# Self and cross attention of a layer as one pipeline of 32 groups, with the query parts on the GpSimd queue

## The reference

```
h  = ln(x) * (1 + scale) + shift            # self attention
q, k, v = split(h @ W_qkv + b)
x += gate * (softmax(q k^T * D**-0.5) v @ W_proj + b)
q  = ln(x) @ W_q + b                        # cross attention, keys and values from the context
k, v = split(context @ W_kv + b)            # layer 1 normalises the context first
x += softmax(q k^T * D**-0.5) v @ W_cproj + b
x += gate_m * mlp(ln(x) * (1 + scale_m) + shift_m)
```

## Time and profile before

| what | value |
|---|---|
| median of 3 runs | 3974.96 us (3955.16 to 3978.48) |
| the profiled execution | 3992.97 us, span 3991.2 us |
| mean granted clock of TensorE | 0.885 of full speed |
| busy: PE, PEld, DVE, ACT, POOL | 83%, 52%, 70%, 54%, 28% |
| DMA, HBM over the span | 164.42 MB moved, HBM 5 GB/s |
| packed attention of layer 1 (self, cross) | 1526 to 1934 us, 1934 to 2338 us |
| packed attention of layer 2 (self, cross) | 2491 to 2899 us, 2900 to 3317 us |

### The profile page before, as it was taken

One profiled execution on the slowest core, in us unless ns is written; L12 is line 12 of the kernel. 1 busy time (PEld: TensorE's weight loads), 2 busy tenths in 40 slices (PEclk: granted clock), 3 DMA queues, 4 the chain that ended last, 5 costly groups with the idle time before them and its releaser, 6 DMA issues. The chain is left out here.

```text
span 3991.2 us, 100093 instructions
## 1 busy us (share of the span) xinstructions
PE 3311.6 (83%) x31675; PEld 2059.8 (52%) x31675; DVE 2802.8 (70%) x12631; ACT 2146.6 (54%) x5112; POOL 1120.2 (28%) x1448
## 2 busy tenths in 40 slices
PE   3999867777777796898699977798879997788998
PEld 2454434444444474555466655465546665545555
DVE  5677689999999784887367568588646757764333
ACT  1566545555555573666256555376625655533443
POOL 2000056666666562111111135111011214410000
PEclk9999978988888796999599879699858978898999
DMA  4000000000000002343134300343223420000000
GB/s 119 13 11 11 11 8 8 8 7 7 8 7 6 1 0 52 98 104 89 45 95 97 83 4 0 81 104 100 59 68 86 100 66 1 22 18 10 14 13 13
DMA packets 138546, 164.42 MB, mean 41 GB/s; under 512 B 40982, under 2 KB 87574, under 8 KB 137750
## 3 DMA queue, kind: packets, MB, share of 16 engines
q1 hardware_dynamic: 119286, 128.40, 12.7%
q0 software_dynamic: 10240, 21.84, 2.4%
q10 hardware_dynamic: 8608, 9.18, 0.9%
HBM read 13.87 MB, written 4.19 MB: 5 GB/s over the span
## 5 line engine op out<-in xcount | busy, mean ns | idle before, releaser
L635 ACT ACTIVATE topk_prob<-topk_s,topk_nmx 128x77 f32<-128x77 f32 x1024 | 248.2, 326 | 320.5 <-POOL topk_nmx L531 213.7
L1224 ACT ACTIVATE cross_pT<-cross_t 77x512 f32<-77x512 f32 x512 | 275.7, 589 | 201.3 <-PE cross_t L1469 201.0
L1333 DVE TENSOR_REDUCE self_mx<-self_s 128x4 f32<-128x512 f32 x512 | 328.8, 684 | 67.5 <-PE self_s L1454 65.1
L1224 ACT ACTIVATE self_pT<-self_t 128x512 f32<-128x512 f32 x512 | 279.0, 600 | 138.9 <-PE self_t L1469 138.9
L1333 DVE TENSOR_REDUCE cross_mx<-cross_s 128x4 f32<-128x308 f32 x512 | 220.3, 472 | 141.2 <-PE cross_s L1454 140.4
L537 POOL TENSOR_SCALAR topk_mask<-topk_work 128x308 f32<-128x308 f32 x256 | 251.5, 983 | 228.1 <-DVE topk_work L778 227.8
L926 PE MATMUL topk_t<-ident,topk_prob 128*77 128x128 f32 x1024 | 189.5, 316 | 147.2 <-POOL topk_prob L541 146.8
L926 PEld LDWEIGHTS topk_t<-ident,topk_prob 128*77 128x77 f32 x1024 | 136.4, 170 | 264.0 <-ACT topk_pT L621 122.2
L916 PE MATMUL topk_s<-kbd,topk_qT 128*128 128x308 f32 x512 | 218.0, 511 | 51.1 <-ACT topk_prob L635 47.4
L1686 POOL TENSOR_TENSOR mlp_hid<-mlp_hid 128x512 fp32r<-128x512 f32 x160 | 210.4, 1315 | 156.1 <-DVE mlp_hid L1759 108.0
L1454 PEld LDWEIGHTS cross_s<-packed_keys,packed_queries 32*128 32x128 f32 x2048 | 159.7, 217 | 133.9 <-issue 80.2
(11 more groups left out here) (333 smaller groups left out, 8710.5 us busy)
## 6 DMA issues: line engine op xcount, KB each, us to landing
packed_keys<-self_kT SPq DMA_DIRECT2D x384, 64.0 KB, 2.1
packed_queries<-self_qT SPq DMA_DIRECT2D x384, 64.0 KB, 2.1
packed_queries<-cross_qT SPq DMA_DIRECT2D x384, 64.0 KB, 2.2
packed_queries<-zero_rows SPq DMA_DIRECT2D x128, 128.0 KB, 2.7
packed_keys<-cross_kT SPq DMA_DIRECT2D x384, 39.0 KB, 1.9
kbd<-window_kT SPq DMA_DIRECT2D x512, 8.0 KB
kbd<-topk_kT SPq DMA_DIRECT2D x512, 4.8 KB
packed_queries<-self_om POOLq DMA_DIRECT2D x128, 64.0 KB, 2.2
```

What stands on the lines that cost most here:

```text
L635: last = nc.scalar.activation(prob[:, u % 4, h * keys:(h + 1) * keys], s_ps[:, u % 2, h * keys:(h + 1) * keys], ACT.Exp, scale=SCALE, bias ...
L1224: nc.scalar.activation(pT[0:keys, c % 2, h, :], t_ps[0:keys, h, :], ACT.Exp, scale=SCALE).then_inc(s_exp, 1)
L1333: nc.vector.tensor_reduce(mx[:, (c // 2) % 2, 2 * k + h, :], sc, AX.X, ALU.max).then_inc(s_max, 1)
```

## The change

`packed_attention_phase(nc, r, layer, kind)` becomes `packed_attention_layer(nc, r, layer)`. One block holds both attentions: there are NT = 32 groups, of which 0 to 15 are the self attention and 16 to 31 the cross attention of the same sequences. `at(n)` gives for a group which attention it is and its number within it. The number of iterations is 32 + 3 where it was 16 + 3 twice.

The query parts move from the SP queue to the GpSimd queue. They are issued in slot 7 of iteration i for group i + 2, behind `stage_context`, and therefore ahead of the `send_maximum` of slot 0 of the next iteration. SP keeps the keys.

On PE, `outputs_to_rows` and `values_times_probs` of the even slots move from right behind the scores to the end of the slot, behind the projections and the unread matmuls. The odd slots keep their order. In the prologue the layer norm of groups 1 and 2 starts before the low parts and the values of the group before it are done. The layer norm statistics of a cross group wait for the addition of the self attention of the same group. The tile of the low and high keys always has the width of the self attention.

```diff
-def packed_attention_phase(nc, r, layer, kind):
+def packed_attention_layer(nc, r, layer):
...
+    NT = 2 * NG
+    def at(n):
+        return (cross_a if n >= NG else self_a), n % NG
...
-            for i in range(NG + 3):
-                body(i, i % 3, i, NG - i)
+            for i in range(NT + 3):
+                body(i, i % 3, i, NT - i)
...
+        def pack_queries(engine, g, buf):
+            engine.wait_ge(s_qlo, g + 1)
+            after(engine, s_st, 2 * NS * (g - 2))
+            for gp in range(2):
+                for p, part in enumerate((0, 1, 0)):
+                    for h in (2 * gp, 2 * gp + 1):
+                        engine.dma_start(r.qp[p:C:4, buf, h, :].bitcast(F32),
+                                         qT[32 * h:32 * h + 32, part, :].bitcast(F32)).then_inc(s_qp[gp], 16)
+                engine.dma_start(r.qp[3:C:4, buf, 2 * gp:2 * gp + 2, :].bitcast(F32),
+                                 r.zero[:, :, :].broadcast_to([32, 2, GT])).then_inc(s_qp[gp], 16)
...
             def prologue():                       # SP
                 for g in range(2):
                     pack_keys(g, g)
-                    pack_queries(g, g)
             def body(i, m3, before, left):
                 if there(before, left, 2):
                     pack_keys(i + 2, (m3 + 2) % 3)
-                    pack_queries(i + 2, (m3 + 2) % 3)
...
             def prologue():                       # GpSimd
-                for g in range(3):
-                    if cross:
-                        stage_context(g)
-                    rstd_of(g)
+                rstd_of(0)
+                rstd_of(1)
+                pack_queries(pool, 0, 0)
+                rstd_of(2)
+                pack_queries(pool, 1, 1)
...
-                    if u == VP and cross and there(before, left, 3):
+                    if u == VP and NG <= i + 3 < NT:
                         stage_context(i + 3)
+                    if u == VP and there(before, left, 2):
+                        pack_queries(pool, i + 2, (m3 + 2) % 3)
...
             def ln_stats(g, bs=range(G)):         # VectorE
+                after(dve, s_x, g - NG + 1)
...
             def prologue():                       # VectorE
                 dve.wait_ge(s_init, n_init)
+                ln_stats(0)
+                ln_variance(0)
+                ln_apply(0)
                 for g in range(2):
-                    ln_stats(g)
-                    ln_variance(g)
-                    ln_apply(g)
+                    ln_stats(g + 1)
+                    ln_variance(g + 1)
                     low_keys(g)
                     low_queries(g)
+                    ln_apply(g + 1)
                     values_out(g, g)
-                ln_stats(2)
-                ln_variance(2)
-                ln_apply(2)
...
-                    dg, c = lagged(u, LV)         # TensorE
-                    if there(before, left, dg):
-                        values_times_probs(i + dg, c, (m3 + dg) % 3)
+                    if u % 2:
+                        values(i, u, m3, before, left)
...
-                    dg, c = lagged(u, LTR)
-                    if c % 2 == 1 and there(before, left, dg):
-                        outputs_to_rows(i + dg, c // 2)
...
+                    if u % 2 == 0:
+                        dg, c = lagged(u, LTR)
+                        if there(before, left, dg):
+                            outputs_to_rows(i + dg, c // 2)
+                        values(i, u, m3, before, left)
...
             for layer in (1, 2):
-                packed_attention_phase(nc, r, layer, "self")
-                packed_attention_phase(nc, r, layer, "cross")
+                packed_attention_layer(nc, r, layer)
                 mlp_phase(nc, r, layer)
```

More of the change, by code:

```diff
@@ L17 @@
 from contextlib import ExitStack
+from dataclasses import dataclass
 import concourse.bass as bass
@@ L1014, in _ @@
             iterations(pe, body, prologue)
-def packed_attention_phase(nc, r, layer, kind):
-    cross = kind == "cross"
-    keys = S if cross else T
-    KW = keys + keys % 2
+@dataclass
+class Attention:
+    cross: bool
+    name_o: str
+    wq: object
+    wk: object
+    wv: object
+    bq: object
+    bk: object
+    bv: object
+    keys: int
+    KW: int
+def packed_attention_layer(nc, r, layer):
+    self_a = Attention(False, f"so{layer}", r.W(f"qkv{layer}", 0), r.W(f"qkv{layer}", C), r.W(f"qkv{layer}", 2 * C),
+                       r.bcol(f"qkv{layer}", 0), r.bcol(f"qkv{layer}", 1), r.bcol(f"qkv{layer}", 2), T, T)
+    cross_a = Attention(True, f"co{layer}", r.W(f"q{layer}"), r.W(f"kv{layer}", 0), r.W(f"kv{layer}", C),
+                        r.bcol(f"q{layer}"), r.bcol(f"kv{layer}", 0), r.bcol(f"kv{layer}", 1), S, S + S % 2)
+    NT = 2 * NG
     NS = 2 * G
@@ L1030, in packed_attention_phase @@
     UNREAD = (2, 3, 2, 2)
[L1031 to L1040, removed]
+    gate, n_gb = dict(GATED)[self_a.name_o], [n for n, _ in GATED].index(self_a.name_o)
+    scale_at, shift_at = SC_A[layer], SH_A[layer]
     source = r.ctxnT if layer == 1 else r.ctxT
+    KW_C = cross_a.KW
+    def at(n):
+        return (cross_a if n >= NG else self_a), n % NG
     with nc.cleanup_on_exit(), ExitStack() as ctx:
-        tag = f"{kind}{layer}_"
+        tag = f"attn{layer}_"
         def sb(name, shape, dtype=F32):
@@ L1057, in packed_attention_phase @@
         xn, hT = sb("xn", [T, G, C]), sb("hT", [C, GT])
[L1058 to L1059 removed]
+        ctxs = sb("ctxs", [C, G * KW_C])
+        qT, kT = sb("qT", [C, 2, GT], F32R), sb("kT", [C, 2, GT], F32R)
         vp = sb("vp", [T, 3, G, 4, 2, 2, 18])
@@ L1082, in packed_attention_phase @@
         s_onps, s_onT, s_pjps, s_pg, s_pgps, s_x = sem("onps"), sem("onT"), sem("pjps"), sem("pg"), sem("pgps"), sem("x")
-        n_init = 4 if cross else 3
+        n_init = 4
         PK, PQ = 16 * 6, 16 * 7
@@ L1108, in pack_keys @@
                         for h in (2 * gp, 2 * gp + 1):
[L1109 to L1120, removed]
+                            sp.dma_start(r.kp[p:C:4, buf, h, 0:G * a.KW].bitcast(F32),
+                                         kT[32 * h:32 * h + 32, part, 0:G * a.KW].bitcast(F32)).then_inc(s_kp[gp], 16)
             def prologue():
@@ L1154, in stage_context @@
             def stage_context(g):
[L1155 to L1163 removed]
+                q = g - NG
+                if q > 0:
+                    pool.wait_ge(s_vps, g)
+                pool.dma_start(ctxs[:, :].rearrange("c (b s) -> c b s", s=KW_C)[:, :, 0:S],
+                               source[:, G * q:G * q + G, :]).then_inc(s_ctx, 16)
+            def prologue():
+                rstd_of(0)
[3 more added lines that the diff above has]
+                pack_queries(pool, 1, 1)
             def body(i, m3, before, left):
@@ L1179, in modulate @@
             def modulate(g, bs=range(G)):
-                if scale_at is None:
-                    if bs[-1] < G - 1:
-                        return
-                    after(act, s_xT, g + 1)
-                    nc.scalar.copy(hT[:, :], l_ps[:, :]).then_inc(s_hT, 1)
+                a, q = at(g)
+                if a.cross:
+                    if bs[-1] == G - 1:
+                        act.wait_ge(s_xT, g + 1)
+                        nc.scalar.copy(hT[:, :], l_ps[:, :]).then_inc(s_hT, 1)
                     return
@@ L1210, in columns_out @@
                 sent = 2 * g + b // 2
-                after(act, s_md[b % 2], 16 * (sent if has_max else min(sent, B // 2)))
+                after(act, s_md[b % 2], 16 * (sent if has_max else min(sent, NT * G // 2)))
                 if has_max:
@@ L1529, in prologue, with values @@
                     project_values(g)
+            def values(i, u, m3, before, left):
+                dg, c = lagged(u, LV)
+                if there(before, left, dg):
+                    values_times_probs(i + dg, c, (m3 + dg) % 3)
             def body(i, m3, before, left):
@@ L1578, in body @@
                             pe.wait_ge(s_onT, g + 1)
-                            nc.tensor.matmul(f_ps[:, :], r.W(name_o), onT[:, :], start=True, stop=True
+                            nc.tensor.matmul(f_ps[:, :], r.W(at(g)[0].name_o), onT[:, :], start=True, stop=True
                                              ).then_inc(s_pjps, 1)
+                    if u % 2 == 0:
+                        dg, c = lagged(u, LTR)
+                        if there(before, left, dg):
+                            outputs_to_rows(i + dg, c // 2)
+                        values(i, u, m3, before, left)
             iterations(pe, body, prologue)
```

71 lines of the change are left out of this document (41 added, 30 removed).

## The result

| | median | range |
|---|---|---|
| kernel before | 3966.61 us (4 runs) | 3955.16 to 3978.48 |
| kernel after | 4160.16 us (4 runs) | 4141.43 to 4176.09 |

The change makes the kernel slower: the ratio is 1.0486, 95% interval 1.0427 to 1.0545. The time lies above the range of the prediction. The profiled execution took 4156.51 us, its span is 4154.7 us and the mean granted clock 0.856, against 0.885 before. Of all runs used here one, at 3864.79 us the slowest of the kernel "half on GpSimd", counts as slow and is not in its ratio; without it that kernel's median is 3832.43 us.

The account below looks back on a forecast made before the run. PE and VectorE were both taken as near full. Loop-bound periods summed to 674.6 us per layer (before 701.1 and 713.9); with 3.8 per prologue, 73 us saved: 3992.97 to 3920, less 18 for the median, 3902; range 3760 to 4090.

Parts of the forecast that it names:

- Part 1: Merging both attention phases of a layer into one pipeline saves 69.1 us in layer 1 and 81.9 in layer 2.
- part 2: Prologue: group 1's layer norm no longer stands behind group 0's values, saving 3.8 us per layer (bounds 0 and 4.9).
- Part 3: PE's even slots: shorter waits for `om`, earlier low queries; up to 1.7 us per self iteration, about 1.1 per cross.
- Part 4: Fourteen query DMAs on GpSimd ahead of slot 3's maximum close a loop: 20.9 us per self iteration, 23.5 cross.
- Loop binds and the clock mostly holds: Likeliest case: the GpSimd query loop sets the periods at mostly full clock; 3902 us, own range 3865 to 3945, chance 0.42.
- the term for falls of the clock: In the summed periods, 0.86 us added per cross iteration for clock falls as now, nothing per self iteration.
- The sign that I had named: Steady self part: a clock under 0.95 would show the prediction wrong, with the time then near 4050 us.
- The rival that came true: PE's stand in slot 3 takes the clock along: mild 4015 us, chance 0.15; severe 4083 us, chance 0.09.
- severe form: Half of each stalled iteration runs at the low clock after slot 3's stand, losing 3.9 us; 4083 us, chance 0.09.
- The normalisations: VectorE's normalisations of x block GpSimd's burst of query issues, losing 36 us; 3938 us, chance 0.05.
- Dear issues: Query issues in a row on GpSimd cost 0.71 us or more each; 4022 us and up, chance 0.08.
- a loop that does not bind: The GpSimd query issues do not hold up PE's slot 3; 3816 us, or down to 3739, chance 0.16.

Follow-up runs that it names:

- half on GpSimd: Changed kernel with seven of the 14 query DMAs (heads 0 and 1) kept on the GpSimd queue and the other seven on SP; 3839.99 us.
- kernel with queries on SP: Changed kernel with all query DMAs issued by the SP queue again; 3763.23 us, ratio 0.9499 to the kernel before.
- stand-filled run: Changed kernel with 10 (self) or 18 (from group 13 on) further unread matmuls ahead of slot 3's waits on PE; 3983.67 us.
- the kernels without the loop: Changed kernel with query DMAs back on SP, 3763.23 us, or on GpSimd in three short blocks behind the maxima of the next iteration, 3759.29 us.

## Why the prediction was wrong

**Part 1 and part 2** were right. I had 151.0 for the merge and 7.6 for the prologue, 158.6 us; measured for both together is 166 (156 to 175 by the interval). The prologue's stand went from 4.92 to 1.14 us, which is the 3.8 taken; what it saved in time was not measured by itself.

**Part 3** was right in kind. The upper bound was 1.7 us in self and 1.1 in cross; the periods moved 1.08 and 0.75. The part that failed is the gain in slot 6: ahead of the query projection PE now waits 1.19 us for the low keys, which read the same PSUM bank, where it had waited 1.12 for `om`. A wait was exchanged, and the low queries come 11.52 us behind slot 3 (1738.50 to 1750.02 in the kernel with queries on SP), where I had 11.0 and the kernel before 12.74.

**Part 4** was right in its mechanism and nearly right in its terms. The issues took 7.35 us for fourteen (7.6 forecast), the wait appeared at slot 3, and it was mostly 1.9 us in self (1.4) and 4.1 to 5.9 in cross (over 3). The self loop at full clock, as estimated above, was 21.8, not 20.9: 0.5 from the low queries, 0.3 from there to the first issue, 0.3 in the landing, less 0.25 in the issues. That is 18 us over 20 self iterations.

**The step that failed** is the choice of the likeliest case, "Loop binds and the clock mostly holds: 0.42", and with it the term for falls of the clock in the sum. I added 0.86 us to a cross iteration for falls of the clock and nothing to a self iteration, because self iterations had stood 0.8 and 1.1 us at full clock. The stands that I forecast were longer than those, and the one fall that I had a row for followed a stretch with PE busy 1.04 of 2 us. By that row alone, over 3 us of standing in every cross iteration should have been the case with most of the chance. It had 0.24 in two forms. The trace of before had more such rows: in that stretch of its cross attention the clock fell in every second iteration, which are those of 21.0 to 22.2 us between those of 19.6. One more of them:

```profile
2153.00:2155.00 2.00, 1.13 (x18) 0.55 (x16) 1.51 (x7) 1.78 (x5) 0.00 (x0) 0.98 0.16 31
2155.00:2158.00 3.00, 2.88 (x20) 1.34 (x20) 0.64 (x3) 1.04 (x3) 0.55 (x1) 0.50 0.46 109
```

In place of 0.86 and nothing the changed kernel lost 6.0 us per cross iteration and 2.1 per self iteration (next paragraph). The difference is 26 x 5.14 + 20 x 2.1 = some 176 us, most of the error of 258. The sign that I had named, a steady self part under 0.95, came (0.90).

**The rival that came true was also too small.** Its severe form gave 4083, from 7 us at the low clock and 3.9 us per stalled iteration. The low clock lasted 33 us after the stand of 4.72 and some 3 to 36 us after the ten long stands. The thirteen cross iterations are 29.3 us each; the loop at full clock is 12.4 + 0.75 + 7.6 + 2.5 = 23.3 (2167.05 to 2190.39, of which only the last 2 us, in the stand, are at the low level). So the falls cost 6.0 us per cross iteration on the mean. In self it is 23.9 - 21.8 = 2.1. That makes an estimated 26 x 6.0 + 20 x 2.1 = 198 us; the stand-filled run puts a floor of 176 us under what the clock cost.

**The normalisations** were given 0.05. The rule that the prediction names from the Trainium skill, SBUF — State Buffer, section "SBUF: two separate sides", by which a GpSimd DMA stands still while VectorE holds the shared port, is not seen here: in the block of issues that starts at 1757.34 VectorE ran two normalisations, by its timeline

```profile
1760.72 0.59 DVE L1328 TENSOR_SCALAR attn_xn<-x_res,attn_mv,attn_rstd 128x128 f32<-128x128 f32 x2
```

and the block took 7.35 us, no more than fourteen single issues. The 768 query issues of the changed kernel have a median of 529 ns and a maximum of 829.

**Dear issues and a loop that does not bind** both fell: 0.52 us each in a row, and the wait was there. The latter case gave 3739 to 3816 for its time, and the kernels without the loop took 3763 and 3759.

## What to carry to other kernels

On an in-order queue the price of a block of cheap DMAs is set by what stands behind it: look for the small transfer that another engine waits for within the same iteration, put the block behind it, and cut it up where the next such transfer would be late too (here 397 us ahead of the wanted maximum, 68 whole behind it, none in three pieces). When a new wait on TensorE is forecast, price it at both clock levels, and look in the profile of before for the shortest stand that was followed by a fall; if the new stand is longer, the fall belongs into the likeliest case, though single longer stands can pass without one (2.54 us with half the queries on GpSimd). Work that fills a stand has a price of its own: before a filled run is read as "the loop without the falls", see whether the wait is still there or the period is the work with the fill. Where a change holds several edits, a large sound gain (here 198 us) can lie under a larger loss, so each edit is worth a run of its own.

## What the runs showed of the hardware

- GpSimd issues in a row are as cheap as single ones, or cheaper: 3.14 us for six DMAs of 64 KB, 0.52 each, against 0.545 alone.
- A stand of PE of 1.9 us can be followed by 6 us at 1.2 GHz (self, changed kernel) or by 21 (cross, half the queries on GpSimd), and a stand need not be followed by any: in the latter kernel PE busy 1.59 of 3 us was followed by 0.50 until 2042, and PE busy 0.71 of 3 us by 1.00.
- After each of the ten stands of 4.1 to 5.9 us in the cross attention of layer 1 of the changed kernel the clock was at 1.2 GHz, for between 3 and 36 us.
- The landing of the same small transfer varies: for the maxima 2.3 to 2.4 us, once 3.7, in the changed kernel, and 2.8 to 4.3 with half the queries on SP. The cause was not isolated. The Trainium skill, DMA: Bandwidth & Descriptors, section "Anatomy of one DMA — SWDGE (gpsimd) path", gives about 2.0 us and the bytes at 436 GB/s, an estimate of 2.15 us for 64 KB. The 2.2 of the earlier trace rows agrees; the landings of 2.8 to 4.3 us do not.
